# Cross-attention with residual and LayerNorm: an opening with a float32 first chunk and deferred shift sums, and a drain that interleaves two token tiles

## The reference, cut to what matters

```python
q = einsum('bte,ef->btf', x, Wq) + bq
k = einsum('bml,le->bme', ctx, Wk) + bk
v = einsum('bml,le->bme', ctx, Wv) + bv
w = einsum('bte,bme->btm', q, k) / sqrt(512)
w = softmax(w, axis=1)               # over the 100 tokens t, for each context row m
pred = einsum('btm,bme->bte', w, v)
y = pred + x
out = (y - mean(y)) * rsqrt(var(y) + 1e-6) * gamma + beta
```

## Time and profile before

| | us |
|---|---|
| median of 3 runs | 144.66 (144.46 to 144.82) |
| the profiled execution | 144.95 |
| its span (first to last instruction) | 143.2 |
| PE busy | 134.4 (94%) |
| DVE busy | 117.3 (82%) |
| ACT busy | 81.6 (57%) |
| POOL busy | 65.2 (46%) |
| granted TensorE clock, mean | 0.992 |

### The profile page before, as it was taken

How to read it: one execution, slowest core, us unless ns; L and a number is a source line. 1 busy time by engine, 2 the same in 40 slices (tenths; PEclk the granted TensorE clock), 3 DMA queues, 4 the chain that set the end, 5 groups by cost and what they waited for, 6 DMA issues and landing times.

```text
span 143.2 us, 2969 instructions
## 1 busy us (share of the span) xinstructions
PE 134.4 (94%) x1046; PEld 129.4 (90%) x1046; DVE 117.3 (82%) x216; ACT 81.6 (57%) x286; POOL 65.2 (46%) x61
## 2 busy tenths in 40 slices
PE   6998999999899999999999999999999999999910
PEld 6998999999898999999999999999999999998900
DVE  0689989999777899759999975899699976876992
ACT  4677349459527836385564729475665628483520
POOL 1000000009031594735758472666667463659891
PEclk9999999999999999999999999999999999999996
DMA  4999999965057597897896889699897886545113
GB/s 141 300 406 421 421 300 395 317 213 194 5 205 237 195 307 243 328 346 259 314 311 259 322 256 402 215 316 326 252 306 250 331 273 225 217 146 178 73 73 146
DMA packets 10670, 37.33 MB, mean 261 GB/s; under 512 B 1184, under 2 KB 1184, under 8 KB 10656
## 3 DMA queue, kind: packets, MB, share of 16 engines
q1 hardware_dynamic: 9424, 34.92, 69.5%
q10 hardware_dynamic: 1232, 2.23, 4.1%
HBM read 33.87 MB, written 3.28 MB: 259 GB/s over the span
## 4 chain that ended last, share of the span: by engine, by line
PE 75%; DVE 10%; DMA 4%; POOL 3%; issue 2%; ACT 2%; SPq 1%; POOLq 1%
PE ps_U L400 28%; PE ps_S L386 27%; PE ps_Y L421 12%; DMA xT_in<-xT 4%; DVE xT_lo L647 3%; PE ps_U L361 3%; DVE xu L659 2%; PE ps_Y L361 2%; POOL xT_in L848 2%; PE ps_w L409 1%; SPq L255 1%; DVE wkq L637 1%; DVE W_lo L744 1%; POOL xT_in L836 1%; POOL rstd L841 1%
## 5 line engine op out<-in xcount | busy, mean ns | idle before, releaser
L521 ACT ACTIVATE expo<-scores,negmax 121x100 f32<-121x100 f32 x96 | 35.0, 366 | 27.3 <-DVE negmax L679 27.3
L386 PE MATMUL ps_S<-G,ctxT_in 128*121 128x100 f32 (+1 forms) x384 | 43.5, 270 | 0.0
L400 PEld LDWEIGHTS ps_U<-prob,ctx_in 121*128 121x128 f32 x360 | 42.1, 192 | 0.9
L400 PE MATMUL ps_U<-prob,ctx_in 121*128 121x100 f32 x360 | 42.5, 274 | 0.0
L386 PEld LDWEIGHTS ps_S<-G,ctxT_in 128*121 128x121 f32 (+1 forms) x384 | 42.0, 185 | 0.0
L825 POOL TENSOR_TENSOR prob<-expo,rinv 121x600 f32<-121x600 f32 x16 | 19.0, 1189 | 35.7 <-DVE rinv L686 35.7
L841 POOL TENSOR_TENSOR rstd<-vareps,neg_half 128x1 f32<-128x1 f32 (+1 forms) x13 | 12.4, 955 | 22.8 <-DVE vareps L717 22.5
L836 POOL TENSOR_TENSOR xT_in<-x_in,xT_in 128x512 f32<-128x512 f32 (+1 forms) x13 | 16.6, 1276 | 13.0 <-issue 8.4
L690 DVE TENSOR_REDUCE probsum<-prob 121x100 f32<-121x600 f32 x16 | 19.8, 1239 | 3.0 <-POOL prob L825 2.7
L521 ACT ACTIVATION_READ_ACCUMULATOR expo<-scores,negmax 121x1 f32 x96 | 18.0, 187 | 0.0
L675 DVE TENSOR_TENSOR scores<-ps_S,c_rows 121x600 f32<-121x600 f32 x16 | 12.5, 782 | 5.8 <-PE ps_S L386 5.6
(11 more groups left out here) (91 smaller groups left out, 175.8 us busy)
## 6 DMA issues: line engine op xcount, KB each, us to landing
ctx_in<-ctx SPq DMA_DIRECT2D x16, 768.0 KB, 5.7
ctxT_in<-ctxT SPq DMA_DIRECT2D x16, 722.0 KB, 5.2
xT_in<-xT SPq DMA_DIRECT2D x8, 400.0 KB, 8.8
x_in<-x SPq DMA_DIRECT2D x12, 256.0 KB, 4.7
out<-xT_in ACTq DMA_DIRECT2D x8, 256.0 KB, 4.2
wqk<-Wqk SPq DMA_DIRECT2D x4, 388.0 KB, 4.3
out<-xT_in SPq DMA_DIRECT2D x3, 256.0 KB, 2.0
wv_in<-Wv SPq DMA_DIRECT2D x1, 512.0 KB, 16.1
```

The source lines that it names most:

```text
L386: last = nc.tensor.matmul(ps_scores(c)[0:rows(c), :], ctxT_in[:, q, l * M + c * MP:l * M + c * MP + rows(c)], G[:, l, bass.ds(b * T, T)], ...
L400: last = nc.tensor.matmul(ps_U[:, q, l * T:(l + 1) * T], ctx_in[0:rows(c), q, c, l * P:(l + 1) * P], prob[0:rows(c), q, c * T:(c + 1) * T] ...
L521: last = nc.scalar.activation(expo[0:MP, q, c * T:(c + 1) * T], scores[0:MP, q, c * T:(c + 1) * T], ACT.Exp, bias=negmax[0:MP, q, c:c + 1] ...
```

## The change

Opening. WARM is 8 instead of 9. The first chunk of W is four float32 matmuls of the raw weights, so its hi and lo parts are not made. The other chunks' `wk_hi` moves from ACT to DVE. In the last chunk the hi lo and lo hi products alternate by output, so that the four outputs end one after another. The second half of x^T of group 0 is rounded by DVE instead of ACT. `project` waits for x^T by halves. The bias sums move from ahead of `project(1)` to after its first block. `sum_shift(1)` moves behind `project(3)`, `sum_shift(2)` behind turn 4 and `sum_shift(3)` behind turn 7, and `weigh_by_u`, `upper_shift`, `lower_shift` and `take_shift` move on their engines.

Drain. U(14) and U(15) are four halves (`late_U`); Y of tile 10 stands between the halves of U(14), Y of tile 11 behind them, then both halves of U(15), and Y of tile 12 in two column halves in different banks. Tile 11 is finished by halves: the right by DVE (`scale_and_shift`), the left by ACT and POOL. Tile 12's y stays in PSUM, its residual is added half by half, and its last step and its stores are halves, on the ACT and SP queues. POOL does `probabilities(15)` ahead of `residual(10)`.

```diff
@@ tensor
-            for f in range(EC):
-                wait_upper_wk(pe, f)
-                pe.wait_ge(wqhi_set, f + 1)
+            pe.wait_ge(w_in[0], 16)
+            for e in range(EC):
+                nc.tensor.matmul(banks[e][:, 0:L + 2], wqT[:, 0, e * P:(e + 1) * P], wkT[:, 0, :], start=True, stop=False)
+            for f in range(1, EC):
+                pe.wait_ge(wkhi_set, f)
+                pe.wait_ge(wqhi_set, f)
...
             project(0)
-            pe.wait_ge(wkq_step, EC)
...
             project(1)
             scores_of(0, 0)
             sum_shift(0)
             project(2)
             scores_of(1, 1)
+            project(3)
             sum_shift(1)
-            project(3)
-            sum_shift(2)
             turn(2, 0)
-            sum_shift(3)
             pe.wait_ge(Wvhi_set, 1)
             pe.wait_ge(Wvlo_set, 1)
-            each_turn(turn, 3)
-
-            weighted_ctx(B - 2, 0)
+            turn(3, 1)
+            turn(4, 0)
+            sum_shift(2)
+            turn(5, 1)
+            turn(6, 0)
+            turn(7, 1)
+            sum_shift(3)
+            each_turn(turn, 8)
...
+            late_U(0)
             weight_sum(NT - 2)
             values(NT - 3)
-            values(NT - 2)
+            late_U(1)
             weight_sum(NT - 1)
...
+            late_U(2)
+            late_U(3)
...
+            last_values(0, 0)
+            last_values(0, 1)
+            last_values(1, 0).then_inc(last_Y_done, 1)
+            last_values(1, 1).then_inc(last_Y_done, 1)
@@ scalar
             take_group(0)
+            upper_half(2)
             upper_shift(0)
-            upper_half(2)
             take_group(1)
             upper_half(3)
-            upper_shift(1)
             take_shift(0)
             exponentials(0, 0)
             take_group(2)
-            upper_shift(2)
+            upper_shift(1)
             act.wait_ge(wv_loaded, 16)
             nc.scalar.activation(Wv_hi[:, :, :], wv_in[:, :, :], ACT.Copy).then_inc(Wvhi_set, 1)
-            take_shift(1)
             exponentials(1, 1)
             take_group(3)
-            take_shift(2)
-            upper_shift(3)
+            take_shift(1)
             act.wait_ge(rows_in, 48)
             upper_U(0, 0)
             exponentials(2, 0)
-            take_shift(3)
+            upper_shift(2)
             value_bias(0)
             exponentials(3, 1)
-            each_turn(turn, 4)
+            turn(4, 0)
+            turn(5, 1)
+            take_shift(2)
+            upper_shift(3)
+            turn(6, 0)
+            turn(7, 1)
+            turn(8, 0)
+            take_shift(3)
+            each_turn(turn, 9)
@@ vector
+            dve.wait_ge(xT_loaded[0][1], 16)
+            nc.vector.tensor_copy(xT_hi[:, 0, EH:, :], xT_in[:, 0, EH:, :]).then_inc(first_xThi_set, 1)
             lower_half(0)
...
             weigh_by_u(0)
+            lower_half(2, (0,))
             lower_shift(0)
-            weigh_by_u(1)
-            lower_half(2)
+            lower_half(2, (1,))
...
             maxima(0, 0)
-            lower_shift(1)
             lower_half(3)
-            weigh_by_u(2)
+            weigh_by_u(1)
             normaliser(0, 0)
             maxima(1, 1)
+            lower_shift(1)
             chunk_sum(0, 0)
-            lower_shift(2)
-            weigh_by_u(3)
             dve.wait_ge(rows_in, 48)
-            lower_shift(3)
             normaliser(1, 1)
             maxima(2, 0)
             lower_U(0, 0)
+            weigh_by_u(2)
             chunk_sum(1, 1)
             normaliser(2, 0)
             maxima(3, 1)
+            lower_shift(2)
             add_residual(0)
             row_stats(0)
             chunk_sum(2, 0)
             centre(0)
-            each_turn(turn, 4)
+            turn(4, 0)
+            weigh_by_u(3)
+            turn(5, 1)
+            turn(6, 0)
+            lower_shift(3)
+            each_turn(turn, 7, B - 1)
...
+            centred_half(NT - 2, 1, centred_set)
+            dve.wait_ge(centred_set, NT - 1)
+            dve.wait_ge(rstd_set, NT - 1)
+            dve.wait_ge(result_set, NT - 3)
+            scale_and_shift(NT - 2, 1, right_result_set)
+
+            q = LAST % 2
+            dve.wait_ge(resid_set, NT)
+            for h in range(2):
+                dve.wait_ge(last_Y_done, h + 1)
+                nc.vector.tensor_tensor(last_y[h], last_Y[h], resid[:, q, halves[h]], ALU.add).then_inc(last_y_set, 1)
+            dve.wait_ge(last_y_set, 2)
+            nc.vector.bn_stats(stats[:, q, :], ps_Y[:, q, :]).then_inc(stats_set, 1)
...
+            for h in range(2):
+                scale_and_shift(LAST, h, last_result_set)
@@ gpsimd
+            probabilities(B - 1, 1)
             residual(NT - 3)
-            probabilities(B - 1, 1)
             residual(NT - 2)
             finish(NT - 4)
             inverse_deviation(NT - 3)
             residual(NT - 1)
             inverse_deviation(NT - 2)
             finish(NT - 3)
-            finish(NT - 2)
+            q = (NT - 2) % 2
+            pool.wait_ge(left_scaled_set, 1)
+            pool.wait_ge(out_stored[q], 16 * ((NT - 2) // 2))
+            nc.gpsimd.tensor_tensor(result[:, q, halves[0]], scaled[:, q, halves[0]], beta_rows[:, halves[0]],
+                                    ALU.add).then_inc(left_result_set, 1)
             inverse_deviation(NT - 1)
```

More of the change, by code:

```diff
@@ L145, in xattn @@
         mask_set = sem("mask_set")
+        first_xThi_set = sem("first_xThi_set")
         xThi_set = sem("xThi_set")
@@ L218, in batch_tokens @@
             return slice(b * T, (b + 1) * T)
+        LAST = NT - 1
+        EHALF = E // 2
+        halves = [slice(h * EHALF, (h + 1) * EHALF) for h in range(2)]
+        last_Y = [ps_Y[:, LAST % 2, 0:EHALF], ps_S[:, 0, 0:EHALF]]
+        last_y = [ps_Y[:, LAST % 2, halves[h]] for h in range(2)]
+        late_parts = [(b, l) for b in (B - 2, B - 1) for l in range(LC)]
         def rows(c):
@@ L231, in first_two, with each_turn @@
             return b < 2
-        def each_turn(turn, first):
-            for b in range(first, B):
+        def each_turn(turn, first, last=B):
+            for b in range(first, last):
                 turn(b, b % 2)
@@ new lines, in _, with bias_sums @@
+            pe.wait_ge(wklo_set, EC - 1)
+            pe.wait_ge(wqlo_set, EC - 1)
+            for e in range(EC):
+                nc.tensor.matmul(banks[e][:, 0:L + 2], wq_hi[:, EC - 1, e * P:(e + 1) * P], wk_lo[:, EC - 2, :],
+                                 start=False, stop=False)
+                nc.tensor.matmul(banks[e][:, 0:L + 2], wq_lo[:, EC - 1, e * P:(e + 1) * P], wk_hi[:, EC - 2, :],
+                                 start=False, stop=True).then_inc(W_summed, 1)
+            def bias_sums():
+                pe.wait_ge(wkq_step, EC)
+                for c in range(LC):
+                    last = nc.tensor.matmul(ps_w[:, c:c + 1], wkq[:, (EC - 1) % 2, c * P:(c + 1) * P], ones[:, 0:1],
+                                            start=True, stop=True)
+                last.then_inc(gbias_summed, 1)
@@ L438, in _ @@
             project(0)
-            pe.wait_ge(wkq_step, EC)
-            for c in range(LC):
-                last = nc.tensor.matmul(ps_w[:, c:c + 1], wkq[:, (EC - 1) % 2, c * P:(c + 1) * P], ones[:, 0:1],
-                                        start=True, stop=True)
-            last.then_inc(gbias_summed, 1)
             project(1)
@@ L485, in _, with last_values @@
             last.then_inc(Y_done, 1)
+            late_U(2)
+            late_U(3)
+            pe.wait_ge(y_set, NT - 2)
+            pe.wait_ge(S_read, B)
+            def last_values(l, h):
+                for upart, vpart in ((U_hi, Wv_hi), (U_hi, Wv_lo), (U_lo, Wv_hi)):
+                    if upart is U_lo:
+                        pe.wait_ge(late_Ulo_set, l + 3)
+                    else:
+                        pe.wait_ge(late_Uhi_set, l + 3)
+                    done = nc.tensor.matmul(last_Y[h], upart[:, l, tokens(LAST)], vpart[:, l, halves[h]],
+                                            start=(l == 0 and upart is U_hi and vpart is Wv_hi),
+                                            stop=(l == LC - 1 and upart is U_lo))
+                return done
+            last_values(0, 0)
+            last_values(0, 1)
+            last_values(1, 0).then_inc(last_Y_done, 1)
+            last_values(1, 1).then_inc(last_Y_done, 1)
         @block.scalar
@@ L782, in _ @@
             centre(0)
-            each_turn(turn, 4)
-            normaliser(B - 1, 1)
-            lower_U(B - 3, 1)
-            lower_U(B - 2, 0)
+            turn(4, 0)
[4 more added lines that the diff above has]
+            each_turn(turn, 7, B - 1)
+            lower_U(B - 4, 0)
+            normaliser(B - 2, 0)
+            maxima(B - 1, 1)
+            add_residual(NT - 4)
+            row_stats(NT - 4)
+            chunk_sum(B - 2, 0)
@@ L787, in _, with scale_and_shift @@
+            def scale_and_shift(j, h, done):
```

(7 more changed lines are left out.)

198 lines of the change are left out of this document (118 added, 80 removed).

## The result

| | before | after |
|---|---|---|
| median, us | 144.75 (6 runs, 144.46 to 145.14) | 149.07 (6 runs, 148.44 to 151.29) |
| profiled execution, us | 144.95 | 149.48 |
| its span | 143.2 | 147.7 |
| mean granted TensorE clock | 0.992 | 0.970 |

After takes 1.0293 times as long as before, with an interval from 1.0264 to 1.0322: 4.2 us slower. The forecast was 149.5. The ratios here leave out every run that is over 1.5% above the fastest of its kernel: 151.29 of after, and the three above 150 of e4 and e5.

What follows compares the result with a forecast made beforehand. PE's work, opening stalls and drain were taken to bound the kernel. Opening -1.5, stalls +2.2 and +3.5 net +4.2; with drain +0.6, 144.95 became 149.75 us profiled, 149.5 median, range 145.6 to 151.6.

Steps and rivals of the forecast that it cites:

- What bounds the kernel: Whole span: PE's work plus opening stalls plus drain; new waits in the steady part are lost, PE having none there.
- Opening: Up to scores(2): earlier project(0) and removed stalls, less a later DVE, gain 1.5 us, between 0.8 and 2.2.
- float32 chunk: First chunk of W: four four-pass matmuls replace twelve one-pass ones, chunk 1 starts as before; counted zero, +-0.2 us.
- The cast on DVE: Opening, ahead of lower_half(0): rounding 800 columns of x^T takes 0.9 us, and PE waits about 0.35 in project(1).
- First stall: Ahead of values(1): weigh_by_u(2) and a held lower_shift(2) lengthen DVE's chain to 10.7 us; PE waits 2.2.
- hold of `lower_shift(2)`: DVE chain to lower_U(1): two SBUF inputs meet POOL's work, so it is held 1.0 us.
- Second stall: From values(1) to values(2): weigh_by_u(3), a POOL hold and two ACT copies make the chain 16.0 us; PE waits 3.5.
- hold by `finish(1)`: Ahead of turn 5: POOL gets in between steps of weigh_by_u(3), and the last step waits 1.25 us.
- Drain: Behind PE's last matmul: POOL's finish(10) holds DVE's scale_and_shift(11, 1) for 1.27 us; net +0.6, or -0.3 if DVE is first.
- (a): Rival: the deferred pieces stall PE, but POOL and DVE don't meet as placed; 147.1 us, chance 0.26.
- (b): Rival: DVE has slack for the deferred pieces, both stalls go, decided in turn 4; 142.9 us, chance 0.12.
- (c): Rival: no difference, opening gains 2.2, meetings cost nothing, stalls of 1.2 and 1.8; 145.5 or 144.7 us, chance 0.06.

Runs made afterwards that it cites:

- e4: The changed kernel with lower_shift(2) moved one place, behind add_residual(0) on DVE; ratio 1.0218 to the kernel before.
- e5: The changed kernel with POOL's finish(10) moved behind its half of tile 11; ratio 1.0234 to the kernel before.
- e1: The changed kernel with all shift work back in the places of the kernel before, new opening and drain kept; 145.28 us, ratio 1.0029.
- e7: The changed kernel with weigh_by_u(2) ahead of maxima(2) and weigh_by_u(3) in steps around maxima(5) and maxima(9), its followers later; 143.53 us, ratio 0.9918.
- e2: The changed kernel with weigh_by_u(2) ahead of maxima(2), weigh_by_u(3) ahead of lower_U(0), two ACT copies behind turn 6; 144.99 us, ratio 0.9994.
- e10: The changed kernel with weigh_by_u(2) ahead of maxima(2), and ACT's take_shift(2) and upper_shift(3) behind turn 6; 146.13 us, ratio 1.0094.
- e11: The changed kernel with weigh_by_u(3) spread in steps, finish(10) moved, and tile 12's y in SBUF instead of PSUM; 143.91 us, ratio 0.9932.

## Why the prediction was right, step by step

**What bounds the kernel: held.** PE was full, and the change won what it removed ahead of it and lost what it put into the steady part. e1 shows that the loss is the order, e7 that it is not the amount.

**Opening: 1.0 instead of 1.5.** The stalls of the earlier trace rows went as worked out in size: from scores(0) to scores(2) it was 16.06 us and is 14.62, less the sum 0.99 (forecast 1.05); that one of them was a meeting with POOL, the working did not see. The term that failed is the float32 chunk, put at 0 and "+-0.2", and with it `project(0)` near 10.7. It started at 11.32, and scores(0) came 0.04 earlier than in before instead of 0.4. The chunk's first row and the first row behind the chunk in after, and the same in e4:

```profile
4.69 1.61 PE L350 MATMUL ps_S<-wqk 128*128 128x258 f32 x4
...
6.82 0.59 PE L355 MATMUL ps_S<-wk_hi,wq_parts 128*128 128x258 f32 x2
```

```profile
4.69 1.10 PE L350 MATMUL ps_S<-wqk 128*128 128x258 f32 x4
...
6.32 0.60 PE L355 MATMUL ps_S<-wk_hi,wq_parts 128*128 128x258 f32 x2
...
8.54 0.48 PE L355 MATMUL ps_S<-wk_hi,wq_parts 128*128 128x258 f32 x2 [0.43 <-ACT wq_parts L639]
```

The chunk took 2.13 us in after, between 1.60 (e2) and 2.76 (e7) elsewhere, by how early PE came to the upper clock level (last section). Chunk 1 thus began at 6.82, 0.48 behind the earlier trace rows; this ate the 0.51 for W_hi. Where the chunk was quick, as in e4 and e2, PE waited 0.43 and 0.50 for a rounding by ACT, which itself waited for the load of its chunk of Wq: `project(0)` began at 11.59 and 11.63. In none of the ten profiled executions with this chunk did it begin ahead of 11.25. The step that failed took W for PE's work alone; behind it stand the clock and the loads.

**The cast on DVE: sized too large.** Forecast 0.9, with waits of 0.35 of PE for xT_lo in `project(1)`. It took 0.58, and no wait came. Its row in after:

```profile
9.83 0.58 DVE L825 CAST xT_hi<-xT_in 128x800 fp32r<-128x800 f32 x1 [0.33 <-DMA xT_in<-xT]
```

The nearest row, the subtraction, was a bad model: 800 columns with one input took little more than the 0.48 that 400 columns of `tensor_scalar` take.

**First stall: 2.08 measured, 2.2 forecast.** The chain from `lower_U(0)` to `lower_U(1)` was 10.59 long (41.03 to 51.62), forecast 10.7. The hold of `lower_shift(2)` was 0.88 (1.45 less 0.57), forecast 1.0, and e4 shows that PE pays it about one for one.

**Second stall: 3.0 undisturbed, 3.5 forecast, and 3.5 in the profiled execution for another reason.** The chain came out right, 15.99 from 51.62 to 67.61 against 16.0, but part of it is PE's slow turn 5. The term that was too large is the hold by `finish(1)`: 0.88 (2.86 less 1.98), forecast 1.25. ACT's copies were 0.81 (e10), forecast 0.85. Without the slow clock after would take some 149.0, and its one run with a mean clock of 0.995 took 149.15.

**Drain: 0.1, forecast +0.6.** What was mis-sized is the time at which DVE gets to tile 12. The hold of `scale_and_shift(11, 1)` came, and in this order, but was 0.9 (1.38 less 0.49, e5), forecast 1.27: POOL had begun 0.34 before DVE. DVE came to tile 12 1.15 behind the start of PE's last matmul, where it was 0.44 and forecast 1.7 (138.0 against 136.28). From there to the store's issue it needed 3.51 instead of 4.06, forecast 3.6. In that stretch the power fell from 0.99 to 0.55, which the forecast had as "no longer late" but not as shorter; e11 shows why. For the landing of a half store no row stood in the forecast; from the last issue to the end of the span it is 2.11 in after and 2.42 in before, 0.3 instead of the 0.2 taken.

**The sum.** -1.0 + 2.1 + 3.5 + 0 against -1.5 + 2.2 + 3.5 + 0.6. The opening was half a microsecond too hopeful, the drain half a microsecond too dear, and the second stall was half a microsecond too dear as well, which the fall of the clock made up in the profiled execution. The mechanisms were right; that the total agrees to half a microsecond is partly luck.

**The rivals.** (a), that the meetings miss, fell: both came, and so did the drain's. (b), that DVE has slack, fell in turn 4 as worked out: the chain was 10.6 long, where 8.4 would have done. But its idea is right at another place: in the earlier trace rows DVE is idle ahead of `lower_U(0)`, and in the turns without `values`; e7 uses just that and is at 143.5, near the 142.9 of (b). (c) fell too: the opening gained 1.0 and not 2.2, and the meetings did cost.

**Not forecast:** the fall of the clock behind a wait. It cost half a microsecond here, and 1.6 where it came at another place (last section).

## What to carry to other kernels

Work that may be done later is not free later: of two places ask each engine's own chain to the next thing PE needs how much it can take, in microseconds, and put there no more than that. Here 2.9 us stood behind `lower_U(0)` with room for 1.6 and cost 2.1 with the hold; with the 2.4 of `weigh_by_u(2)` ahead of `maxima(2)`, where DVE was idle, the wait was gone. The other piece cost nothing once it was cut into steps over two short turns. When DVE and POOL both have SBUF operands, look for those that the same event releases, and in a tail let the short instruction that is waited for go first, or give DVE an operand in PSUM.
